# Two stacked matmuls for the last input tile of the first deep layer, and pair 0 fed straight from the gathered rows

## The reference, cut to what matters

```python
emb = tables[feat_idx, sparse]                      # (512, 26, 32)
linear_out = lin_sparse_w[feat_idx, sparse].sum(-1) + dense @ lin_dense_w
x0 = xk = emb
for w, bb in ((conv1_w, conv1_b), (conv2_w, conv2_b)):
    hp = einsum('bhd,bmd->bhmd', xk, x0)            # products of features
    xn = sigmoid(einsum('oi,bid->bod', w, hp.reshape(-1, h * 26, 32)) + bb)
    xk, half = xn[:, :64], xn[:, 64:]               # 128 outputs each
    res.append(half)
cin_out = concat(res, 1).sum(-1) @ cin_w + cin_b
deep_x = concat([emb.reshape(-1, 832), dense], -1)  # 845 inputs
h1 = tanh(deep_x @ W1 + b1)                         # 1024
h2 = tanh(h1 @ W2 + b2)                             # 512
h3 = tanh(h2 @ W3 + b3)                             # 256
y = linear_out + cin_out + (h3 @ deep_w + deep_b) + bias
```

## Time and profile before

| | |
|---|---|
| median of 3 launches | 415.51 us (414.73 to 419.06) |
| the profiled execution's own time | 415.48 us |
| its span, first to last instruction | 413.6 us |
| TensorE busy | 400.0 us, 97% |
| VectorE busy | 311.5 us, 75% |
| DMA moved | 74.14 MB, mean 179 GB/s |

### The profile page before, as it was taken

One profiled execution on the slowest core, in us unless ns is written; L12 is line 12 of the kernel. 1 busy time (PEld: TensorE's weight loads), 2 busy tenths in 40 slices (PEclk: granted clock), 3 DMA queues, 4 the chain that ended last, 5 costly groups with the idle time before them and its releaser, 6 DMA issues.

```text
span 413.6 us, 5230 instructions
## 1 busy us (share of the span) xinstructions
PE 400.0 (97%) x1854; PEld 167.1 (40%) x1854; DVE 311.5 (75%) x345; ACT 160.7 (39%) x267; POOL 169.6 (41%) x146
## 2 busy tenths in 40 slices
PE   3999979999999999999999999999999999999997
PEld 1432323333333333333333333333333335887885
DVE  4019579899898989898989889898989897442123
ACT  3074334544544544435353544544443601111012
POOL 6763572654856654826655700000000355780000
DMA  5249689999999999899999999999967760420000
GB/s 206 43 98 237 165 206 239 236 245 234 254 246 226 241 217 235 215 226 225 225 244 220 231 226 237 202 225 212 229 158 200 202 156 14 115 76 2 0 0 3
DMA packets 42177, 74.14 MB, mean 179 GB/s; under 512 B 20593, under 2 KB 23025, under 8 KB 42150
## 3 DMA queue, kind: packets, MB, share of 16 engines
q1 hardware_dynamic: 38566, 72.03, 71.4%
q0 software_dynamic: 3584, 1.76, 2.9%
...
## 4 chain that ended last, share of the span: by engine, by line
PE 84%; DMA 7%; POOL 4%; issue 2%; SPq 1%; DVE 1%; ACT 0%; DVEq 0%
PE conv L494 42%; PE conv L472 17%; PE conv L515 8%; PE ring L515 7%; PE ring L484 5%; POOL emb L395 4%; PE ring L454 4%; DMA emb<-in_table,rows 2%; DMA laid<-emb 1%; DMA copied<-laid 1%; DMA raw<-laid 1%; PE ring L530 1%; SPq L332 1%; DMA idx_sb<-in_idx 0%; DVE copied L835 0%
## 5 line engine op out<-in xcount | busy, mean ns | idle before, releaser
L395 POOL DMA_INDIRECT emb<-in_table,rows x112 | 137.2, 1225 | 98.0 <-DMA emb<-in_table,rows 66.3
L835 DVE TENSOR_TENSOR copied<-copied,xk 128x1024 f32<-128x1024 f32 x112 | 135.4, 1242 | 5.6 <-DMA copied<-laid 5.6
L835 DVE TENSOR_TENSOR prod<-ring,xk 128x1024 f32<-128x1024 f32 x96 | 113.9, 1214 | 31.3 <-ACT xk L661 30.8
L494 PE MATMUL conv<-copied,w_sb 128*64 128x512 f32 x448 | 105.5, 594 | 1.2 <-DVE copied L835 1.1
L494 PE MATMUL conv<-prod,w_sb 128*64 128x512 f32 x384 | 93.1, 605 | 0.9 <-DVE prod L835 0.9
L661 ACT ACTIVATE xk<-conv,const_sb 64x512 f32<-64x512 f32 x64 | 43.6, 682 | 124.7 <-PE conv L472 123.8
L472 PE MATMUL conv<-sq,w_sb 117*64 117x512 f32 x384 | 88.1, 593 | 0.3 <-ACT sq L690 0.3
L494 PEld LDWEIGHTS conv<-copied,w_sb 128*64 128x64 f32 x448 | 31.6, 137 | 65.4 <-issue 52.0
L650 ACT ACTIVATE sq<-ring 117x512 f32<-117x512 f32 x90 | 48.4, 596 | 4.7 <-PE ring L454 4.0
L404 POOL TENSOR_TENSOR xt_lo<-xt,xt_hi 128x512 fp32r<-128x512 f32 (+1 forms) x7 | 10.9, 1578 | 94.6 <-ACT xt_hi L727 90.0
L472 PEld LDWEIGHTS conv<-sq,w_sb 117*64 117x64 f32 x384 | 27.2, 136 | 54.2 <-issue 53.9
...
## 6 DMA issues: line engine op xcount, KB each, us to landing
copied<-laid SPq DMA_DIRECT2D x224, 256.0 KB, 5.2
...
```

The lines of the kernel that those rows point to most:

```text
L395: pool.indirect_dma_start(out=emb[0:n, i, j, :], out_offset=None, in_=table, in_offset=bass.IndirectOffsetOnAxis(ap=rows[0:n, i, j:j + 1], ...
L494: mm = nc.tensor.matmul(conv[i % 2][c * HALF:(c + 1) * HALF, :], w2_sb[:, t, :], prod_of(r)[:, c, :], start=(t == 0), stop=(t == T2 - 1))
L835: nc.vector.tensor_tensor(prod_of(r)[:, :, :].rearrange("p c n -> p (c n)"), left[:, :, :].rearrange("p c n -> p (c n)"), xk[i % 2][:, :, ...
```

## The change

1. The seventh input tile of layer 1 is stacked. Its rows are now 64 feature rows and three copies of the 13 dense rows (at 64, 77 and 96, `KB` = 109 rows in all). The first matmul multiplies `m1_hi`, whose 64 feature rows a DMA has doubled into rows 64 to 127 (`twice_in`), with the high and the low part of the features: hi by hi and hi by lo, 128 rows. The second multiplies a `m1_lo` that also holds minus the high part of the dense weights with an `xt_hi` that holds minus the high part, the high part and minus the low part of the dense inputs, 109 rows. So it takes two matmuls instead of three. The parts for it are made by two new VectorE instructions in pair 15 after tile 5 (`LAST_AT`), one GpSimd instruction that reads rows 0 to 63 and writes 64 to 127, and three small DMAs more for each of the last two pieces of W1.
2. Pair 0 no longer comes back from DRAM for `x`: `DIRECT` = 1 lets seven DMAs copy the gathered rows inside SBUF into a buffer (`direct`), each as soon as its gather has landed, two ScalarE and two VectorE instructions make `x` from it, and `fetch(0)` is gone.
3. Pair 0 has five copied tiles (3, 6, 7, 8, 11) and eight spread ones. The sixth buffer gets tile 2 of pair 1.
4. `lay_out(2)` stands before the fifth of the first copies, `fetch(2)` before the sixth. `x_low(2)` stands after tile 11. `WARM` is 9.

```diff
@@ constants
-K1_LAST = ML * E + ND
+KF = ML * E
+DENSE_ROWS = (KF, KF + ND, KF + 32)
+KB = DENSE_ROWS[2] + ND
 WP = 512
 DENSE_AT = 96
 ...
+DIRECT = 1
 XEND = HALF + XK
 RING = 3
 RP = 3
 COPIED = (2, 3, 6, 7, 8, 11, 12)
-SPREAD = tuple(t for t in range(T2) if t not in COPIED)
-NC, NS = len(COPIED), len(SPREAD)
+COPIED_0 = (3, 6, 7, 8, 11)
 RC = 6
 ...
-
-C_B1, C_B2, C_B3, C_DEEP, C_CB1, C_CB2, C_CIN1, C_CIN2, C_ONE, C_AUX, C_LOW, C_END = 0, 8, 12, 14, 16, 17, 18, 19, 20, 22, 23, 24
+LAST_AT = 5
+X_LOW_AT, TURN_AT, FOLD1_AT, PIECE_AT = (11, 5), 9, (5, 5), 11
+WARM = 9
 ...
@@ tables of the order
@@ -210,6 +213,10 @@
                     mlp3[j * P:(j + 2) * P, :].rearrange("(k p) n -> p k n", p=P),
                     m3_hi[:, j:j + 2, :], m3_lo[:, j:j + 2, :])
 
+        def piece_landed(k):
+
+            return 16 * (k // 2 + 1 + (len(DENSE_ROWS) if k // 2 >= K1 - 1 else 0))
+
         def wait_rows(eng, i):
 
 ...
 
+        copy_tiles = list(COPIED_0) + [T2 * i + t for i in range(1, NPAIR) for t in COPIED]
+        copy_number = {r: n for n, r in enumerate(copy_tiles)}
+        spread_tiles = [r for r in range(NTILE) if r not in copy_number]
 ...
-        enter(("spread", SPREAD[0]))
-        enter(("spread", SPREAD[1]))
+        first = [r for r in spread_tiles if r < T2]
+        second = [r for r in spread_tiles if T2 <= r < 2 * T2]
+        for r in first[:3]:
+            enter(("spread", r))
         for u in range(UT):
             enter(("sums", 1, u))
-        for r in SPREAD[2:]:
+        for r in first[3:]:
             enter(("spread", r))
         for k in range(2):
             enter(("sums", 2, k))
-            enter(("spread", T2 + SPREAD[k]))
+            enter(("spread", second[k]))
         for i in range(1, NPAIR):
@@ SyncE
+                if k // 2 == K1 - 1:
+                    at = k % 2 * WP
+                    sp.dma_start(wpiece[k % 2][0:KF, :], mlp1[(K1 - 1) * P:(K1 - 1) * P + KF, at:at + WP])\
+                      .then_inc(piece_in[k % 2], 16)
+                    for q in DENSE_ROWS:
+                        sp.dma_start(wpiece[k % 2][q:q + ND, :], mlp1[M * E:M * E + ND, at:at + WP])\
+                          .then_inc(piece_in[k % 2], 16)
+                    return
                 dst, src, _, _ = piece(k)
                 sp.dma_start(dst, src).then_inc(piece_in[k % 2], 16)
 ...
-            fetch(0)
             lay_out(1)
             fetch(1)
-            for n in range(RC):
+            for n in range(4):
                 copy(n)
             lay_out(2)
+            copy(4)
             fetch(2)
-            sp.dma_start(xt[ML * E:K1_LAST, K1 - 1, :], dense_t).then_inc(dense_in, 16)
+            copy(5)
+            sp.wait_ge(xt_zero, 1)
+            for q in DENSE_ROWS:
+                sp.dma_start(xt[q:q + ND, K1 - 1, :], dense_t).then_inc(dense_in, 16)
             for i in range(NPAIR):
                 if i < KW:
                     load_piece(i)
-                for k in range(NC):
-                    n = NC * i + RC + k
+                for k, n in enumerate(copies_of(i)):
                     if k == FETCH_AT and i + RX < NPAIR:
                         fetch(i + RX)
-                    if n < NC * NPAIR:
-                        copy(n)
+                    if n + RC < len(copy_tiles):
+                        copy(n + RC)
                     if k == LAY_AT and i + RX < NPAIR:
                         lay_out(i + RX)
+                if i == NPAIR - 2:
+                    sp.wait_ge(piece_lo, KW)
+                    sp.dma_start(m1_hi[KF:2 * KF, K1 - 1, :].bitcast(F32),
+                                 m1_hi[0:KF, K1 - 1, :].bitcast(F32)).then_inc(twice_in, 16)
             for k in range(KW, PIECES):
                 load_piece(k)
@@ GpSimd
-                n = P if k < K1 - 1 else K1_LAST
                 pool.wait_ge(xt_hi_done, k + 1)
-                nc.gpsimd.tensor_tensor(xt_lo[0:n, k, :], xt[0:n, k, :], xt_hi[0:n, k, :].bitcast(F32),
+                if k == K1 - 1:
+                    pool.wait_ge(xt_lo_done, K1 - 1)
+                    nc.gpsimd.tensor_tensor(xt_lo[KF:2 * KF, k, :], xt[0:KF, k, :], xt_lo[0:KF, k, :].bitcast(F32),
+                                            ALU.subtract).then_inc(xt_lo_done, 1)
+                    return
+                nc.gpsimd.tensor_tensor(xt_lo[:, k, :], xt[:, k, :], xt_hi[:, k, :].bitcast(F32),
                                         ALU.subtract).then_inc(xt_lo_done, 1)
 
 ...
@@ TensorE, deep(): the last input tile
                         pe.wait_ge(h_lo_done, start - kt + k + 1)
-                    r = K1_LAST if layer == 0 and k == K1 - 1 else P
+                    if layer == 0 and k == K1 - 1:
+                        if n == 0:
+                            pe.wait_ge(twice_in, 16)
+                            pe.wait_ge(last_step, 2)
+                        nc.tensor.matmul(MLP_BANKS[n % 2], hi[:, k, mt * P:(mt + 1) * P], xl[:, k, :],
+                                         start=False, stop=False)
+                        mm = nc.tensor.matmul(MLP_BANKS[n % 2], lo[0:KB, k, mt * P:(mt + 1) * P], xh[0:KB, k, :],
+                                              start=False, stop=True)
+                        continue
                     for j, (w, h) in enumerate(((hi, xh), (lo, xh), (hi, xl))):
-                        mm = nc.tensor.matmul(MLP_BANKS[n % 2], w[0:r, k, mt * P:(mt + 1) * P],
-                                              h[0:r, k, :], start=(k == 0 and j == 0),
+                        mm = nc.tensor.matmul(MLP_BANKS[n % 2], w[:, k, mt * P:(mt + 1) * P],
+                                              h[:, k, :], start=(k == 0 and j == 0),
                                               stop=(k == kt - 1 and j == 2))
                 if ks is None or ks[-1] == kt - 1:
@@ TensorE, the order of pairs 0 and 1
-            spread_tile(SPREAD[0])
-            spread_tile(SPREAD[1])
+            for r in first[:3]:
+                spread_tile(r)
             layer1(0, 1)
             pe.wait_ge(w2_in, 16)
-            slot_free("sums", 1, 0)
+            pe.wait_ge(l1_read, 1)
             for k in range(2):
-                nc.tensor.matmul(sums_bank(1, 0)[:, 0, :], w2_sb[:, 0:2, :].rearrange("p t o -> p (t o)"),
+                nc.tensor.matmul(conv[0][:, :], w2_sb[:, 0:2, :].rearrange("p t o -> p (t o)"),
                                  w2_sb[:, 0:8, :].rearrange("p t o -> p (t o)"), start=True, stop=True)
             main(0)
             main(1)
             for u in range(UT):
                 sums_of(1, u)
             main(2)
-            spread_tile(SPREAD[2])
+            spread_tile(first[3])
             main(3)
-            spread_tile(SPREAD[3])
+            spread_tile(first[4])
             layer1(1, 0)
-            for r in SPREAD[4:-1]:
+            for r in first[5:]:
                 spread_tile(r)
             for t in range(4, 8):
                 main(t)
-            spread_tile(SPREAD[-1])
             layer1(1, 1)
             for t in range(8, T2 - 1):
                 main(t)
-            for k in range(2):
-                sums_of(2, k)
-                spread_tile(T2 + SPREAD[k])
+            sums_of(2, 0)
+            spread_tile(second[0])
             main(T2 - 1)
+            sums_of(2, 1)
+            spread_tile(second[1])
             for i in range(1, NPAIR):
                 for g, tiles_now in enumerate(GROUPS):
@@ ScalarE
                     act.wait_ge(turned, 2 * NPAIR)
-                    act.wait_ge(dense_in, 16)
-                    for k in range(K1):
-                        n = P if k < K1 - 1 else K1_LAST
-                        nc.scalar.activation(xt_hi[0:n, k, :], xt[0:n, k, :], ACT.Copy).then_inc(xt_hi_done, 1)
+                    for k in range(K1 - 1):
+                        nc.scalar.activation(xt_hi[:, k, :], xt[:, k, :], ACT.Copy).then_inc(xt_hi_done, 1)
+                    nc.scalar.activation(xt_lo[0:KF, K1 - 1, :], xt[0:KF, K1 - 1, :], ACT.Copy)\
+                      .then_inc(xt_hi_done, 1)
 
             sigmoid2(NPAIR - 1)
@@ VectorE
                 dve.wait_ge(piece_hi, k + 1)
+                if k // 2 == K1 - 1:
+                    nc.vector.scalar_tensor_tensor(lo, src, small_sb[0:KB, C_TAKE:C_TAKE + 1], hi.bitcast(F32),
+                                                   ALU.mult, ALU.subtract).then_inc(piece_lo, 1)
+                    return
                 nc.vector.tensor_tensor(lo, src, hi.bitcast(F32), ALU.subtract).then_inc(piece_lo, 1)
 
 ...
             nc.vector.tensor_scalar(w1a_sb[:, :, :], w1b_sb[:, :, :], 0.5, None, ALU.mult).then_inc(w1_step, 1)
 ...
                         fold2_of(i - 1)
+                    if t == LAST_AT and i == NPAIR - 1:
+                        dve.wait_ge(dense_in, 16 * len(DENSE_ROWS))
+                        dve.wait_ge(l1_done, 2 * NPAIR)
+                        dve.wait_ge(turned, 2 * NPAIR)
```

(10 more changed lines are left out.)

45 lines of the change are left out of this document (24 added, 21 removed).

## The result

The changed kernel takes 419.51 us (median of 20 runs, 417.68 to 421.55), the kernel before 415.69 beside it: a ratio of 1.0086, 95% interval 1.0071 to 1.0101. It is slower, by 3.8 us between the medians and 3.6 by the ratio. I had forecast 415.3, with 418.2 as the upper end of the range. The profiled execution took 419.52 us, with a span of 417.7 against 413.6.

What follows compares the result with a forecast made beforehand. TensorE was taken to be saturated once the sums of pair 3 can begin, a moment set by the gather chain. On 415.48 us: start +0.5, pair 15 +1.1, stacked tile -1.82, giving 415.3; range 411.8 to 418.2.

Steps and rivals of the forecast that it cites:

- The stacked tile, -1.82: Layer 1: one matmul of 0.2277 us less in each of eight output tiles, 1.82 us off.
- GpSimd's seventh low part: Pair 15: it writes another half of the partitions, at the price of the other low parts.
- The two VectorE instructions, +1.1: Pair 15: they take 1.2 us, less VectorE's lead of 0.1, so TensorE waits 1.1 us more at the last tiles.
- the lock that the Trainium skill describes: Pair 15: the new subtraction could wait for the rest of a GpSimd instruction; covered by the upper bound of 1.5 us.
- The start, +0.5: Start of the run: the first sums of pair 3, at 63.97 us before, come 0.5 us later.
- 0.5 us earlier: Start: gathers of pair 2 end this much sooner beside four copies in place of six, between nothing and 1.5.
- two gathers of seven at the light pace: Start, pair 3's gathers: two at 1.5 us, five at 2.4, a step of 15.0 us, 1.0 more than before.
- some 3 us: Start: TensorE's wait before the sums of pair 3, from its earlier start 2.6 and the gaps 0.62 and 0.39.
- a fall of the clock at 1.9: Rival: idling before pair 3's sums brings back the 1.2 GHz level, 1.9 us more, 417.2 us; chance 0.15.
- the two slower rivals: Start: pair 3's gathers beside copies all the time, 417.6 us, and the lower clock, 417.2 us; chance 0.15 each.
- both slower rivals at once: Whole run: what a time over 419.7 us, slower by over 1%, would take; chance 0.04.
- First sums of pair 0 near 18.8: Start, a sign to look for: these sums, at 21.41 us before, come at about 18.8 with three warm-ups less.

Runs made afterwards that it cites:

- e7: The kernel before with the stacked tile alone (old start), its two new VectorE instructions behind tile 12 of pair 15: 413.86 us, ratio 0.9958 to the kernel before.
- c2: The changed kernel with nothing altered, run as a control on the same chip: 419.95 us, ratio 1.0113 to the kernel before.
- e2: The changed kernel with three matmuls for the last input tile again, so only the new start is left: 425.81 us, ratio 1.0073 to the kernel before.

## Why the prediction was wrong

**The stacked tile, -1.82: right.** -0.24 and -1.59 in the trace, and e7 measured 0.9958 where the term alone gives 0.9956. One reading beside it was off and cost nothing: GpSimd's seventh low part took 2.06 us, not the 1.28 of the others, and was done at 348.82, well ahead of its use at 352.46.

**The two VectorE instructions, +1.1: right**, measured +1.21, with some luck in the size. VectorE had no lead left, as read; e7 takes the term away by a place where nobody waits behind them. But the two took 1.46 us, not 1.2, and the three products behind them took 3.50 in place of 3.80. The multiply is what was long: 0.73, with a GpSimd instruction under way until 339.43, against 0.48 in e7, with none. The new subtraction took 0.69 in both. GpSimd did nothing while it ran (its next instruction starts at 344.04), so the lock that the Trainium skill describes for two inputs in SBUF (SBUF — State Buffer, "SBUF: two separate sides") was not put to the test by it.

**The start, +0.5: the failed step.** It measured +2.63, by two errors in it, and by 0.48 from a chain that began later, for which I had no term:
- The gathers of pair 2, "0.5 us earlier" beside four copies in place of six. The step was 15.0 us as before (14.9), and on chip 8 it was 14.6 in e7 and 14.9 in c2. The DMA share says why: the two copies that were moved had run mostly behind these gathers, not beside them. From 30 to 38 us the share is 1.04 before and 1.02 in the changed kernel, so full in both. The rows of pair 2 have landed at 38.27 before (their `lay_out`), and only behind that do the kernels differ: 1.02 from 38 to 42 before, 0.32 in the changed kernel.
- The gathers of pair 3, "two gathers of seven at the light pace" and five at the heavy one, 15.0 us. It was 16.4, near the heavy end. The first gathers did meet nearly idle DMA engines (0.32 from 38 to 42), as I had it. But I gave each gather a price of its own, and what counts is the landing of the last one: 7.3 us behind its issue, against 4.9. Before, the lull stood in front of it, from 42 to 48, around the `fetch` of pair 2 at 44.41 and not only after it. That this alone makes the difference is argued from the traces, not shown.

**The idle gap, and the clock: the second failed step.** The forecast itself had TensorE wait "some 3 us" ahead of pair 3, and priced a fall of the clock at 1.9 in a rival with a chance of 0.15. Its own terms give more than 3: 2.6 + 0.62 + 0.39 is 3.6, and with the sums 0.5 later it is 4.1. The wait was 7.07: TensorE was there at 59.53, 4.05 earlier than before (I had 2.6 + 0.6), and the sums 2.63 later. Not one gap of the kernel before had gone, but three, those of 0.62, 0.41 and 0.46 between 53 and 60. The clock then fell from 1.00 to 0.52 and cost 2.2 to 2.4 us, close to my 1.9. The size was right and its weight wrong: the clock stood at 0.50 from 62 us on, with the last matmul at 59.53, so that in this trace a wait of the 4.1 us that my terms add up to would have met it too. The Trainium skill (TensorE: Matmul & The Clock Gate, "HAM oscillation — how this bites in real kernels") describes a wait for DMA after which the array runs at half rate; the trace agrees, with 3.68 us for eight matmuls in place of 1.94. I treated the two slower rivals as exclusive, but one feeds the other: later sums make the wait longer. 415.48 + 2.6 + 2.2 + 1.2 - 1.8 = 419.7, and 419.52 was measured; "both slower rivals at once" had 0.04 where it was the likely case once the gathers were late.

**"First sums of pair 0 near 18.8":** they came at 19.30, still 2.1 earlier, and that gained nothing, as said: it only made the wait longer.

**What stays open:** that the new start as a whole loses is shown (e7 beside c2, and e2). That the order of the postponed copies, and no other part of the new start, makes the step of pair 3 long rests on two pairs of traces; the experiments meant to undo it fell on chips that cover it. The seven direct copies of pair 0 are an untested rival. So is the price of arriving early: no run has the changed kernel with twelve warm-ups, which would shorten the wait. The clock's share rests on rows of three kernels with an idle stretch ahead of the lower clock, not on a run with the wait filled. Why ScalarE stops on some chips isn't known.
